# Context attention with keys on partitions, scores in 32-row groups, 1024-wide exponentials, and three chunks in flight in one order

## What is computed

```python
x = x + attn(_layernorm(x), ...)                     # 8 heads of 64, 2048 keys
# context attention, q from x, k and v from the 128 context tokens
qh = _split_heads(q @ Wq + bq)                       # 16 heads of 32
kh = _split_heads(k @ Wk + bk)
vh = _split_heads(v @ Wv + bv)
logits = jnp.einsum('bhqd,bhkd->bhqk', qh, kh) * scale
weights = jax.nn.softmax(logits, axis=-1)
out = jnp.einsum('bhqk,bhkd->bhqd', weights, vh)
x = x + concat(out) @ Wo + bo
x = x + ffn(_layernorm(x), ...)                      # top 2 of 8 experts, gelu
```

## Time and profile before

| | |
|---|---|
| time, median of 3 runs | 2671.47 us (2669.42 to 2675.68) |
| the profiled execution | 2669.74 us, its span 2668.1 us |
| TensorE busy | 2347.0 us, 88% |
| VectorE busy | 1885.0 us, 71% |
| ScalarE busy | 1573.4 us, 59% |
| GpSimd busy | 1451.8 us, 54% |
| mean granted TensorE clock | 0.953 |

### The profile page before, as it was taken

How to read it: one execution, slowest core, us unless ns; L and a number is a source line. 1 busy time by engine, 2 the same in 40 slices (tenths; PEclk the granted TensorE clock), 3 DMA queues, 4 the chain that set the end, 5 groups by cost and what they waited for, 6 DMA issues and landing times. The chain is left out here.

```text
span 2668.1 us, 67265 instructions
## 1 busy us (share of the span) xinstructions
PE 2347.0 (88%) x22736; PEld 1357.0 (51%) x22736; DVE 1885.0 (71%) x2895; ACT 1573.4 (59%) x2658; POOL 1451.8 (54%) x1007
## 2 busy tenths in 40 slices
PE   5887999999986898869968879999999878887699
PEld 2443666666653555524434436666666535554244
DVE  6996777777846787752269977787777467877532
ACT  3544888888884445521134458888888844455210
POOL 5765888888883220140057658888888832211300
PEclk9997999999998999879989989999999989999799
DMA  3000000000002000030030000000000120000300
GB/s 83 28 8 1 9 5 3 8 8 8 8 18 71 17 17 1 1 75 28 28 92 24 8 1 9 8 4 4 8 8 8 32 56 17 17 1 1 79 24 31
DMA packets 68944, 57.30 MB, mean 21 GB/s; under 512 B 41682, under 2 KB 41682, under 8 KB 68818
## 3 DMA queue, kind: packets, MB, share of 16 engines
q1 hardware_dynamic: 68818, 55.70, 9.2%
HBM read 47.21 MB, written 8.39 MB: 21 GB/s over the span
## 5 line engine op out<-in xcount | busy, mean ns | idle before, releaser
L659 POOL TENSOR_TENSOR probs_l<-probs,probs_h 128x1024 f16<-128x1024 f32 x448 | 981.6, 2213 | 189.5 <-PE bank L711 151.6
L777 DVE TENSOR_REDUCE pm<-bank 128x1 f32<-128x512 f32 x1024 | 671.8, 686 | 197.2 <-PE bank L667 187.5
L771 ACT ACTIVATE probs<-bank 128x1024 f32<-128x1024 f32 x512 | 524.3, 1024 | 126.3 <-POOL probs_l L659 55.3
L763 ACT ACTIVATE probs_h<-bank 128x1024 f16<-128x1024 f32 x512 | 522.1, 1020 | 55.5 <-PE bank L683 55.4
L667 PE MATMUL bank<-ko,q_hh 128*128 (+1 forms) x1024 | 396.1, 390 | 34.1 <-DVE pm L777 22.7
L682 PE MATMUL bank<-q_hh,ko 128*128 (+1 forms) x1024 | 391.5, 382 | 26.6 <-DMA q_lm<-nm 17.4
L683 PE MATMUL bank<-q_lm,k_h 65*128 (+1 forms) x1024 | 391.6, 382 | 0.0
L696 PE MATMUL bank<-v_hl,probs_h 128*128 (+1 forms) x4096 | 326.7, 192 | 0.3
L696 PEld LDWEIGHTS bank<-v_hl,probs_h 128*128 128x128 f16 x4096 | 288.3, 98 | 65.8 <-issue 8.7
L698 PE MATMUL bank<-v_hl,probs_h 128*128 (+1 forms) x4096 | 319.4, 193 | 0.0
L894 POOL TENSOR_SCALAR rs_d<-mv_d 128x1 f32<-128x1 f32 x64 | 21.8, 340 | 512.1 <-DVE mv_d L905 512.1
(11 more groups left out here) (189 smaller groups left out, 4807.9 us busy)
## 6 DMA issues: line engine op xcount, KB each, us to landing
xt_a<-in_x SPq DMA_DIRECT2D x32, 256.0 KB, 2.7
xr<-in_x SPq DMA_DIRECT2D x32, 256.0 KB, 3.0
stage_f<-in_L_ffn_W SPq DMA_DIRECT2D x32, 256.0 KB, 4.8
out<-yt_f SPq DMA_DIRECT2D x32, 256.0 KB, 2.0
q_lm<-nm SPq DMA_DIRECT2D x256, 0.2 KB, 4.9
v_hl<-in_L_attn_w_q SPq DMA_DIRECT2D x8, 256.0 KB, 7.0
v_hl<-in_L_attn_w_k SPq DMA_DIRECT2D x8, 256.0 KB, 8.0
v_hl<-in_L_attn_w_v SPq DMA_DIRECT2D x8, 256.0 KB, 9.6
```

Source lines behind the costliest of these rows:

```text
L659: pool.tensor_tensor(probs_l[:, p % 2, :], probs[:, p % 2, :], probs_h[:, p % 4, :], ALU.subtract).then_inc(pl_pool, 1)
L763: act.activation(probs_h[:, p % 4, :], SB[p % 2][:, :], ACT.Exp).then_inc(ph_ready, 1)
L771: act.activation(probs[:, p % 2, :], SB[p % 2][:, :], ACT.Exp).then_inc(p_ready, 1)
L777: dve.tensor_reduce(pm[:, k:k + 1], MB[k % 2], AX_X, ALU.max).then_inc(mx_free, 1)
```

## The change

Keys lie on partitions in the scores, so the exponentials come out as the values product needs them and no transpose of probabilities or queries is left.

- Queries are projected with features on partitions (`query(c, d)`, d = 4 groups of 4 heads). ScalarE writes their high part and a float32 copy, GpSimd the low part (`query_low`).
- The maximum over the keys is made as before from tokens on partitions, from high parts alone: `maxima(c, d)`, four matmuls and four reductions. `max_rows` turns the negated maxima onto partitions in four small matmuls.
- `scores(c, g)`: 16 matmuls of 32 rows and 512 columns. Part 0 to 2 are high x high, low key x high, high x low; part 3 adds the maxima with a selector `sel`. Four heads have a bank each and a row group each (`tile_position`).
- `exponentials(c, k)`: two exponentials of 1024 columns for a unit k of two heads, one to fp16 and one to fp32. `probs_low` is on GpSimd.
- `values(c, k)`: 24 matmuls of 33 or 32 columns; the 33rd column of `vtab` is one and gives the sum. `output` divides.
- The layer norm of both residuals is applied on ScalarE inside the loop; GpSimd makes a third small step (`rs[:, 2]`) for its bias.
- x is loaded into its place in `x2`, not into `xr`, and a chunk's load waits for no residual. For chunk 0 it is issued behind the weight pieces.
- Body c holds the end of chunk c - 1 (`x`), the units of chunk c, and the start of chunk c + 1 (`y`): "three chunks in flight". The turns of the two `TB` banks and of the two `PB` banks are one list each.

```diff
-                    kbl = sb(ph, "kbl", [P, DC, 4 * CTX], F16)
-                    vxh = sb(ph, "vxh", [P, D], F16)
-                    vxl = sb(ph, "vxl", [P, D], F16)
+                    kth = sb(ph, "kth", [P, DC, CTX], F16)
+                    ktl = sb(ph, "ktl", [P, DC, CTX], F16)
+                    vtab = sb(ph, "vtab", [P, XH, XW], F16)
+                    sel = sb(ph, "sel", [P, DC, P], F16)
...
+                    def norm_scale(pool, s, c, j):
...
+                        pool.wait_ge(d_rs[s], n * TPC + j + 1)
+                        pool.nop(nofuse=True)
+                        pool.tensor_scalar(rs[:, 2, k:k + 1], mv[:, k, 0:1], rs[:, 1, k:k + 1], -1.0, ALU.mult, ALU.mult)\
+                            .then_inc(d_nb[s], 1)
...
+                        BODY_P = [("xo", X, 0), ("mt", 0, 0), ("op", Y, 0), ("xo", X, 1), ("op", Y, 1), ("xo", X, 2),
+                                  ("op", Y, 2), ("xo", X, 3), ("op", Y, 3)] + QUERY_P
...
+                            def probs_low(c, k):
+                                u = (b * CH + c) * 8 + k
+                                pool.wait_ge(d_p32, u + 1)
+                                if (c, k) >= (0, 2):
+
+                                    pool.wait_ge(d_av_done, u - 1)
+                                pool.tensor_tensor(pxl[:, k % 2, :], px[:, k % 2, :], pxh[:, k % 2, :], ALU.subtract)\
+                                    .then_inc(d_pl, 1)
...
+                            def maxima(c, d):
+                                n = b * CH + c
+                                pe.wait_ge(d_qh, n * DC + d + 1)
+                                for j in range(TPC):
+                                    pe.matmul(bank_free("sm", c, 4 * d + j), qh[:, d, j * P:(j + 1) * P], kbh[:, d, :],
+                                              start=True, stop=True).then_inc(d_sm_done, 1)
...
+                            def scores(c, g):
+                                n = b * CH + c
+                                pe.wait_ge(d_mt, n + 1)
+                                pe.wait_ge(d_ql, n * DC + g + 1)
+                                if c or g:
+
+                                    pe.wait_ge(d_o, (n * DC + g) * 2)
+                                for part in range(4):
+                                    for a in range(4):
+                                        rows = slice(32 * a, 32 * a + 32)
+                                        left = (kth, ktl, kth, sel)[part][rows, g, :]
+                                        right = mt[rows, :] if part == 3 else (ql if part == 2 else qh)[rows, g, :]
+                                        mm = pe.matmul(SB[a][:, :], left, right, start=(part == 0), stop=(part == 3),
+                                                       tile_position=(32 * a, 0))
+                                        if part == 3:
+                                            mm.then_inc(d_s_done if a == 3 else d_s_part, 1)
+
+                            def values(c, k):
+                                g, half = k // 2, k % 2
+                                n = b * CH + c
+                                pe.wait_ge(d_pl, n * 8 + k + 1)
+                                bank = SB[2 * half]
...
+                                if y:
+                                    transposes("t5", c + 1, 3)
+                                    attn_project(c + 1, 2)
+                                values(c, 1)
+                                if x:
+                                    cross_project(c - 1, 3)
+                                scores(c, 1)
...
+                            def exponentials(c, k):
+                                g, half = k // 2, k % 2
+                                u = (b * CH + c) * 8 + k
+                                act.wait_ge(d_s_done, (b * CH + c) * DC + g + 1)
+                                if (c, k) >= (0, 2):
+
+                                    act.wait_ge(d_av_done, u - 1)
+                                act.activation(pxh[:, k % 2, :], pairs[half][:, :], ACT.Exp).then_inc(d_ph, 1)
+                                act.activation(px[:, k % 2, :], pairs[half][:, :], ACT.Exp).then_inc(d_p32, 1)
```

More of the change, by code:

```diff
@@ L226, in decoder_layer @@
         d_xb2 = sem("d_xb2")
-        d_bn, d_stat, d_var, d_rs = ([sem(f"{name}{s}") for s in range(2)] for name in ("d_bn", "d_stat", "d_var", "d_rs"))
+        d_bn, d_stat, d_var, d_rs, d_nb = ([sem(f"{name}{s}") for s in range(2)]
+                                          for name in ("d_bn", "d_stat", "d_var", "d_rs", "d_nb"))
         d_n0 = sem("d_n0")
         d_n1 = sem("d_n1")
-        d_q = sem("d_q")
         d_o = sem("d_o")
@@ new lines, in max_rows @@
+                            def max_rows(c):
+                                n = b * CH + c
+                                pe.wait_ge(d_nm, n * 16 + 16)
+                                bank = bank_free("mt", c, 0)
+                                for j in range(TPC):
+                                    mm = pe.matmul(bank[:, j * P:(j + 1) * P], nmt[:, j, :], ident16[:, :],
+                                                   start=True, stop=True)
+                                mm.then_inc(d_mt_done, 1)
@@ new lines, in _ @@
+                            for j in range(TPC):
+                                transposes("t0", 0, j)
+                            query(0, 0)
+                            query(0, 1)
+                            maxima(0, 0)
+                            query(0, 2)
+                            maxima(0, 1)
+                            query(0, 3)
+                            maxima(0, 2)
+                            maxima(0, 3)
+                            for c in range(CH):
+                                body(c)
@@ L1320, in _ @@
+                            layer_norm(1, CH - 1, 2)
+                            layer_norm(1, CH - 1, 3)
+                            for j in range(TPC):
+                                high("t3", CH - 1, j)
                         @block.vector
                         def _(dve):
-                            def low(before, i, dst, high):
-                                dve.wait_ge(d_th, before + i + 1)
-                                dve.tensor_tensor(dst, TB[i % 2][:, :], high, ALU.subtract).then_inc(d_tl, 1)
@@ new lines, in _ @@
+                            for j in range(TPC):
+                                low("t0", 0, j)
+                            for d in range(DC):
+                                maxima(0, d)
+                            for c in range(CH):
+                                body(c)
+                            low("t2", CH - 1, 0)
+                            low("t2", CH - 1, 1)
+                            residual2(CH - 1, 0)
+                            residual2(CH - 1, 1)
+                            low("t2", CH - 1, 2)
@@ L1457, in decoder_layer @@
+                            low("t2", CH - 1, 3)
+                            residual2(CH - 1, 2)
+                            residual2(CH - 1, 3)
+                            for j in range(TPC):
+                                low("t3", CH - 1, j)
                 with ExitStack() as ph:
```

884 lines of the change are left out of this document (514 added, 370 removed).

## The result

The changed kernel takes 2834.70 us, the median of four runs (2831.53 to 2842.41), the kernel before 2672.22 (2669.42 to 2675.68). The ratio is 1.0613, with a 95% interval of 1.0598 to 1.0627: slower by 163 us. The forecast was 2798 with a range of 2690 to 2885. The profiled execution took 2831.53 us, its span 2830.1.

The account below looks back on a forecast made before the run. TensorE, busy 88% of the span, was taken as the bound, with the new order adding waits. 2669.74 + 67 (loop) + 60 (low clock) = 2797, or 2798 us on the median's scale; own range 2730 to 2850, 8 in 10 2690 to 2885.

Parts of the forecast that it names:

- TensorE's work: Full-clock TensorE work in a middle chunk of the context loop: 50.7 us, 11.8 less than before.
- V0, V1 and V2: TensorE waits at the first three two-head units' values, behind GpSimd's subtraction: 3.2, 5.5 and 5.0 us a middle chunk.
- V3: TensorE wait at the fourth unit's values, behind two bias additions and a subtraction on GpSimd: 2.3 us.
- The first query: TensorE wait at a chunk's first query projection, for ScalarE's last high and low part: 2.9 us.
- Low clock: Full-speed work lost in the context loop after TensorE's waits: 7.5 us a chunk, 60 us in all.
- The ends: Loop of a batch outside its middle chunks: start 27 us, chunk 0 73, chunk 3 50.8, tail 25, before low clock.
- by the same steps: Chunk 0, without half of an earlier chunk, estimated with the middle chunk's steps: 73 us.
- Edits at nothing: Edits such as later x loading, selector copies and changed tensors, mostly outside the loop, taken to change no time.
- serial scores: Rival: 32-row score matmuls go one after another, 9.8 us more a chunk, 2876 us; chance 0.13.
- No change: Rival: middle-chunk waits of 28 us and no more clock lost, 2671 us; chance 0.04.
- faster (2577): Rival: middle-chunk waits stay at 16.1 us, each chunk falls by 11.8 us, 2577 us; chance 0.16.
- TensorE's work decides: Rival: TensorE's reduced work sets the loop's time, 11.8 us less a chunk, 2577 us; chance 0.16.

Follow-up runs that it names:

- e3: Changed kernel with GpSimd's subtractions ahead of scale steps and ScalarE's first exponentials ahead of normalisations, same instructions: 2709.94 us.
- e2: Changed kernel's order with dummy matmuls, read by nobody, put into TensorE's waits in the context part: 2798.12 us.
- e5: Changed kernel with all 16 score matmuls of a step reading rows 0 to 31 in row group 0: 2981.57 us.
- e8: e3 with the last chunk and tail reordered, its subtractions on VectorE, and the maxima's matmuls writing the two transpose banks: 2688.48 us.
- e1: Changed kernel with the two score loops swapped, so four matmuls of one row group follow each other: 2839.77 us.
- e6: e3 with dummy matmuls at the ends of the loop and ahead of the first query: 2693.75 us.
- e10: e9 with dummy matmuls in the waits at the loop's ends and ahead of the first query: 2663.38 us.
- e9: e8 with the fourth query transpose ahead of third scores, its copy ahead of their exponentials, and the last reduction behind the last output: 2663.75 us.

## Why the prediction was right, and where its sum was off

The direction, the mechanism and the range held; the forecast was 37 us low. Its own steps:

- **TensorE's work.** The score matmuls were taken at 4.0 us a chunk and took 3.9. But the 50.7 us of a chunk were too few: e3's chunk has 70.67 us, 14.2 of waits, so 56.5 of work at a clock of 0.98, about 55.5 at full speed. Part of the missing 5 us is a drain that a wait's length does not show: a matmul that another follows costs 0.216 us, the last one ahead of a wait its whole 0.38. With 19 waits that is 3.1 us. Another 0.8 is the change of tiling, below; the last 1 us I did not trace.
- **Waits.** V0, V1 and V2 were predicted at 3.2, 5.5 and 5.0 and measured at 3.04, 5.46 and 5.03; each of them sits behind the scale step for the reason given. V3 (2.3) did not appear in a middle chunk. The first query 2.9, measured 2.68; the maxima 7.2, measured 5.0 in the chunk's window (2.9 and 2.1), 5.4 with the queries' own waits. The 30.7 us were 26.3, 4.4 too many.
- **The sum of the two** was 81.4 us, and e2's middle chunk, at a clock of 0.99, took 83.20. The two errors cancelled. This chunk was right partly by luck.
- **Low clock.** 7.5 us a chunk, measured 8.4. The middle chunks of batch 1 took 88.67 and 88.71 us against 81.4 + 7.5 = 88.9, those of batch 0 about 3 more.
- **The ends.** This is the term that was mis-sized. Start and chunk 0 were taken at 27 + 73, 107.5 with the clock; from 836.45 to 949.39 they took 112.9. Chunk 3 and the tail were 50.8 + 25, 83.3 with the clock, and took 91.2 (1133.11 to 1224.35). That is 5.4 + 7.9 us of the 18.9 by which batch 0's loop (387.9) exceeds the 369 of the sum; the middle chunks (183.7 for 163 + 15) are the other 5.7. Batch 1's loop exceeds it by 11.1. In chunk 0 the step "by the same steps" failed: TensorE has no earlier chunk's half, comes to V0 sooner and waits there 8.34 us instead of 3.2. In the tail the third projection waits 4.56 us for a copy that is queued behind two normalisations on ScalarE, which the 25 us did not hold. Without the clock the last chunk and its tail are 15.4 us over the 75.8, 9.0 in the eight units and 6.4 in the tail.
- **Edits at nothing.** Outside the loops there is a difference of 161.8 - 157.1 = 4.7 us. The loop of batch 0 starts 1.05 us later than before (836.45 for 835.40); the rest I did not trace.

The rivals: serial scores are excluded by e5, which shows what they would look like. No change and faster (2577) fell with the waits of the middle chunk, 26.3 us where the turning point was put at 28: on waits alone it would have been nearly even, and it is the work I had missed, the clock and the ends that made it slow. "TensorE's work decides" was the right picture of a kernel that did not exist yet: in e3 the middle chunk fell by 7.9 us against the 11.8 of that rival.

Three rules of the Trainium skill were weighed. The Trainium skill, TensorE: Matmul & The Clock Gate, section Measured speedup vs the span model, gives 3.07x for four row tiles; here 16 took 0.97 us against 3.56 in one row group (e5), which is 3.7x. For this sequence, four deep in each row group, the measurement decides. The Trainium skill, TensorEngine Tiling (Array Packing), section Key Properties, has a drain at a change of tiling mode. In e3's timeline the last projection starts at 957.88 and the first scores at 958.20, and the last scores at 958.85 and the transposes at 959.17:

```profile
957.88 0.38 PE L160 MATMUL bank<-dwh_xo,xol 128*128 128x512 f16 x1
958.20 0.39 PE L1299 MATMUL bank<-qh,kth 32*128 32x512 f16 x4
...
958.85 0.38 PE L1299 MATMUL bank<-mt,sel 32*128 32x512 f16 x4
959.17 0.66 PE L1229 MATMUL bank<-ident,ko 128*128 128x128 f32 x4
```

Each is 0.32 us. Where one step follows another at full clock in the changed kernel and neither the tiling changes nor a bank is waited for, it is 0.21 to 0.23, so a change costs 0.10 us, eight of them 0.8 us a chunk. With that rule the trace agrees, and the price is small. The Trainium skill, TensorEngine Tiling (Array Packing), section PSUM Bottleneck, says that the emptying of the banks may bound once tiling has made TensorE faster. Here it was not the main loss: TensorE waited 1.1 us in the middle chunk for the banks of the tiled scores. The maxima, which are not tiled, were paced by their reductions in any bank (e8), at 2.9 us a chunk.

## What to carry to other kernels

An in-order queue that holds both a latency-bound small step and a long step on the critical chain should have the long one first where it is ready: the same instructions in another order were worth 125 us here. When a change deepens a software pipeline, work out its first and last iterations by their own waits, since a steady state that is 8 us faster per chunk can still lose if four chunks are all there are. And price each wait of TensorE with what comes behind it: its drain, and the work that then runs at the lower clock.

## What was not expected of the hardware

- Matmuls in different row groups ran beside each other even where four of the same group stood together in the program (e1): 16 took the same 1.0 us in either order, and the thirteenth started before the second.
- In one row group, 32-row matmuls of 512 columns took 0.22 us each at full clock and 0.43 at half: no faster than 128 rows.
- Going into row tiling and out of it cost 0.10 us each.
- Filling waits with dummies raised the clock to 0.99 in a middle chunk and gave 37 us in one order, 16 in another and nothing in a third, so it is no general remedy. From the first values of the last chunk to the end of the loop, a clock of 0.82 for 0.73 (e6) came with 2.1 us more and 0.87 for 0.70 (e10) with 1.5 us less.
- In a stretch of 8 us where e9 and e10 have the same instructions, ahead of the first dummy, the clock was 1.00 in one execution and 0.57 in the other, worth 1.7 us.
